# A recurrent attention layer on one core: two TensorE steps change places around the first chunk's scores

## The reference: what is computed

```python
h = rmsnorm(xn) * qkv_norm_w
q, k, v = split(h @ quantised(qkv_w).T)          # 16 heads of 64
for each chunk of T = 128 tokens:                # in order, with a state S per head
    scores = (q_i @ k_i.T) * mask                # decay mask, lower triangle
    o      = scale * (scores @ v_i + (q_i * lam_t) @ S)
    S      = lam_T * S + (k_i * lam_rev).T @ v_i
out = rmsnorm(rmsnorm(o) ...) @ quantised(proj_w).T
g   = silu(xn @ quantised(ffn_w).T + bias)
result = x + out * g
```

## Time and profile before

| | before |
|---|---|
| median of 3 runs | 1341.33 us (1341.18 to 1342.14) |
| the profiled execution: its own time | 1341.38 us |
| its span, first to last instruction | 1340.1 us |
| PE busy | 1312.0 us, 98% |
| DVE, POOL, ACT busy | 934.7, 635.5, 583.5 us |
| mean granted TensorE clock | 1.000 of full speed |

### The profile page before, as it was taken

How to read it: one execution, slowest core, us unless ns; L and a number is a source line. 1 busy time by engine, 2 the same in 40 slices (tenths; PEclk the granted TensorE clock), 3 DMA queues, 4 the chain that set the end, 5 groups by cost and what they waited for, 6 DMA issues and landing times.

```text
span 1340.1 us, 25937 instructions
## 1 busy us (share of the span) xinstructions
PE 1312.0 (98%) x10409; PEld 842.5 (63%) x10409; DVE 934.7 (70%) x1489; ACT 583.5 (44%) x1139; POOL 635.5 (47%) x532
## 2 busy tenths in 40 slices
PE   4999999999999999999999999999999999999998
PEld 2577767674656657566675656657566575656655
DVE  7887467785666957667575776957667686776835
ACT  5884143343434544444353434544344453434521
POOL 1432877952544535447341654535435352654432
PEclk9999999999999999999999999999999999999999
DMA  9521111203021030300303021030301303020000
GB/s 363 234 95 64 72 33 38 97 17 119 2 71 64 17 118 1 121 15 17 118 17 118 2 96 40 17 119 1 127 9 21 114 17 119 1 88 17 33 32 32
DMA packets 33432, 90.32 MB, mean 67 GB/s; under 512 B 10529, under 2 KB 10785, under 8 KB 33314
## 3 DMA queue, kind: packets, MB, share of 16 engines
q1 hardware_dynamic: 33024, 88.65, 18.7%
q10 hardware_dynamic: 290, 0.02, 0.0%
HBM read 71.85 MB, written 16.81 MB: 66 GB/s over the span
## 4 chain that ended last, share of the span: by engine, by line
PE 89%; POOL 3%; DVE 3%; ACT 2%; issue 2%; DMA 1%; SPq 0%; POOLq 0%; ACTq 0%; DVEq 0%
PE ring L747 19%; PE ring L880 15%; PE ring L706 13%; PE ring L732 12%; PE ring L680 11%; PE att_ps L784 4%; PE att_ps L830 3%; PE att_ps L834 3%; PE ring L796 2%; PE att_ps L811 2%; PE ring L759 1%; POOL sq L2186 1%; PE ring L655 1%; DMA raw<-in_ffn_w 1%; ACT junk L1700 1%
## 5 line engine op out<-in xcount | busy, mean ns | idle before, releaser
L747 PE MATMUL ring<-b_lo,qkv_q 128*128 128x256 f16 x1216 | 268.2, 273 | 0.0
L747 PE MATMUL ring<-b_hi,qkv_q 128*128 128x256 f16 x1216 | 268.2, 272 | 0.0
L880 PE MATMUL ring<-proj_q,o_hi 128*128 128x512 fp8e4 x496 | 188.1, 379 | 3.0 <-DVE o_lo L1422 3.0
L880 PE MATMUL ring<-proj_q,o_lo 128*128 128x512 fp8e4 x496 | 188.0, 379 | 0.0
L2142 POOL TENSOR_TENSOR gate_even<-gate_even,bias 128x512 f32<-128x512 f32 x14 | 19.8, 1414 | 275.4 <-ACT gate_even L1819 275.4
L2182 POOL TENSOR_TENSOR sq<-sq,cols 128x1024 f32<-128x1024 f32 x29 | 55.1, 1900 | 165.5 <-DVE b_lo L1254 157.3
L747 PEld LDWEIGHTS ring<-b_hi,qkv_q 128*128 128x128 fp8e4 x1216 | 120.3, 99 | 15.6
L747 PEld LDWEIGHTS ring<-b_lo,qkv_q 128*128 128x128 fp8e4 x1216 | 118.9, 98 | 15.7
L2208 POOL TENSOR_TENSOR xt<-xt,gate_even 128x512 f32<-128x512 f32 x58 | 88.2, 1531 | 69.7 <-DVE gate_even L1442 68.5
L2186 POOL TENSOR_TENSOR sq<-sq 128x1024 f32<-128x1024 f32 (+1 forms) x58 | 109.5, 1888 | 4.5
L1843 ACT ACTIVATE gate_even<-gate_even 128x512 f32<-128x512 f32 x60 | 37.6, 629 | 154.7 <-DVE gate_even L1285 154.7
(11 more groups left out here) (257 smaller groups left out, 3249.1 us busy)
## 6 DMA issues: line engine op xcount, KB each, us to landing
xt<-in_x SPq DMA_DIRECT2D x62, 512.0 KB, 8.3
out<-xt SPq DMA_DIRECT2D x31, 512.0 KB, 3.1
raw<-in_qkv_w SPq DMA_DIRECT2D x24, 512.0 KB, 15.7
y<-in_x_turned SPq DMA_DIRECT2D x14, 512.0 KB, 6.8
y_odd<-in_x_turned SPq DMA_DIRECT2D x14, 512.0 KB, 7.7
raw<-in_ffn_w SPq DMA_DIRECT2D x8, 512.0 KB, 9.9
norm_rows<-norm_out SPq DMA_DIRECT2D x14, 256.0 KB, 6.0
raw<-in_proj_w SPq DMA_DIRECT2D x6, 512.0 KB, 4.5
```

The costliest lines, as they stand in the source:

```text
L747: ins = pe.matmul(ring[:, b, e * BT:(e + 1) * BT], qkv_q[:, cb, o:o + P], part[:, cb, :], start=(cb == 0 and part is b_hi), stop=(cb == NC ...
L880: ins = pe.matmul(ring[:, b, :], part[:, cb, :], proj_q[:, cb, cs], start=(cb == 0 and k == 0), stop=(cb == NCB - 1 and k == 1))
```

## The change

Two calls in TensorE's program change their places in blocks 3 to 15; no instruction is added or taken away, and no other engine's program changes.

```diff
                 last = is_last(chunk(i, c))
                 scores(i, c)
                 if c == 0:
-                    v_product(i, "p4")
+
+                    turn_k(i, 1)
                     product(i, "p1")
-                    turn_k(i, 1)
                 else:
...
                 turn_k(i, 0)
                 v_product(i, "p3")
                 v_product(i, "p7")
+                v_product(i, "p4")
                 attention_by_tokens(i, 0)
                 attention_by_tokens(i, 1)
```

## The result

The changed kernel takes 1361.88 us (median of 5 runs, 1360.72 to 1364.09) against 1341.18 us for the kernel before on the same chip (5 runs, 1340.94 to 1342.14): a ratio of 1.0154, 95% interval 1.0142 to 1.0165. The forecast was 1358.3 us, with a range up to 1361.5. So the direction is right, and the time lies 0.4 us above the range and 3.6 us above the forecast. The profiled execution took 1361.88 us itself, 20.5 us more than that of before.

The account below looks back on a forecast made before the run. TensorE's list of matmuls was taken to set the time (busy 1312.0 of 1340.1 us). Hold 13.1, edges 0.1, POOL waits 2.6 and 1.1 made 16.9 us on 1341.4: 1358.3 us, range 1354 to 1361.5.

Parts of the forecast that it names:

- The hold at p4: TensorE's p4 right after p7 waits for DVE's add_v: 1.01 us in each of thirteen blocks, 13.1 us.
- The edges: TensorE's steps between kinds of matmul, p7 to outputs: 0.01 us a block, 0.1 us in all.
- POOL's chain: Later p1 delays sq_sum at L857: 2.6 us in three long waits, 1.1 us in six small ones.
- What I cost at nothing: Mask, ACT's take_v before the transposes' second half, and squares before chunk 1's scores: no new waits, 0 us.
- The sum: Whole kernel: 13.1 + 0.1 + 2.6 + 1.1 = 16.9 us on 1341.4, giving 1358.3 us, 1.3% slower.
- the hold is there: Denies the rival that ready scores pass the waiting p4 on TensorE, without hold: 1344.0 us, chance 0.03.
- the edges give nothing back: Denies the rival of scores beside transposes and p1 to outputs each 0.09 us cheaper: 1356.0 us, inside the range.
- the waits for `o_lo` are untouched: Denies the rival that the hold swallows TensorE's waits for o_lo and sq_sum: 1349.3 us, chance 0.04.
- POOL is late everywhere: Rival at L857: upper bound of POOL's chain, 6.2 us, with upper hold 14.3: 1362.0 us, chance 0.07.

Follow-up runs that it names:

- turning alone: Only the turning of k put ahead of p1, p4 left behind the scores, against the kernel before: 1353.35 us, ratio 1.0088.
- first try at a better version: Kernel before with POOL's sum_squares(i, 0) earlier, decay_state for chunk 1 behind output_scale(i, 0), and DVE's scale_o(i, 0) ahead of take_z21: 1345.94 us.
- before, squares first: Kernel before with POOL's squares of chunk 0 ahead of its decay of q for chunk 1, blocks from 3 on: 1345.07 us, ratio 1.0027.
- changed, squares first: Changed kernel with POOL's squares of chunk 0 ahead of its decay of q for chunk 1, blocks from 3 on: 1366.36 us, ratio 1.0185.
- before, second operation halved: Kernel before with two small POOL operations, the second at half its columns, ahead of sq_sum in blocks 4, 8 and 12: 1346.11 us, ratio 1.0037.
- `p4` alone, second operation halved: Kernel before with only p4 ahead of the scores, plus two small POOL operations, the second at half columns, ahead of sq_sum: 1362.14 us, ratio 1.0154.
- before, two small operations: Kernel before with two small POOL operations added ahead of sq_sum in blocks 4, 8 and 12: 1350.26 us, ratio 1.0058.

## Why the forecast was right in direction and too low in size

**The hold at p4** was right: 1.00 us in block 8 for 1.01, thirteen waits, 11.0 us of idle as foretold. Moving `p4` alone, which shifts no other wait, measured 13.5 us for the 13.1 of this term, inside its bounds.

**The edges** were mis-sized. Scores to transposes took the 1.99 us that I took, but the transposes behind the scores take 0.93 us in place of the 0.88 that they take behind a v product. With 1.06 us a block in all, hold and edges come to 13.8 us for 13.2.

**POOL's chain** was right, both for the three long waits (0.89 more each for 0.87) and for the six small ones (0.15 us for 0.18): 3.6 us for 3.7. Blocks 3, 7, 11 and 15 kept their margin.

**What I cost at nothing** held. The turning alone shows how near it was: without the scores as cover the wait for `take_v` costs 7 us.

**The sum** is the step that failed, by a term that it lacks. I let each wait cost what it lasts. I had read a granted clock of 1.00 and took it as given, while I put waits of 1.64 us in the place of waits of 0.77. After the longer ones the clock falls to a half for 3.41 us, in one to three blocks of a run, at 1.7 us each. In the changed kernel's five runs the clock shows one fall (1360.72 us), two (1361.50, 1361.88 and 1362.09) and three (1364.09). Take 1.7 us off for each, and the five are 1358.1 to 1359.0, against a forecast of 1358.3. The run with one fall lies inside the range, so it hung on the number of falls on which side of 1361.5 the median came.

That a longer wait at L857 does this is shown from both sides: lengthened without holds, it brings falls; shortened with all holds in place, the clock stays at 1.000 and the time drops by 7.0 us. None of the rivals came to pass: the hold is there, the edges give nothing back, the waits for `o_lo` are untouched, and POOL is late in six of the ten other blocks by 0.15 us, not in all. The measured time lies near that of "POOL is late everywhere" (1362.0) by accident; its reason is not in the trace.

Open is why one wait of 1.66 to 1.70 us is followed by a fall and the next is not, and whether the holds have a share at these lengths. What the runs show is how often. The table counts falls over all runs of a kernel, by clock and time; the waits are those of its profiled execution. Long waits had falls more often, and at about equal length the kernels with holds had more.

| kernel | waits | holds | falls, of waits |
|---|---|---|---|
| first try at a better version | 1.27 us at L880 | no | 0 of 28 |
| before, squares first | 1.54 us at L868 | no | 0 of 21 |
| changed, squares first | 1.55, 1.56 us at L868 | yes | 0 of 15 |
| turning alone | 1.64, 1.65 us at L857 | no | at most 2 of 12 |
| changed | 1.63, 1.66 us at L857 | yes | 10 of 15 |
| before, second operation halved | 1.66 to 1.70 us at L857 | no | 7 of 15 |
| `p4` alone, second operation halved | 1.68, 1.69 us at L857 | yes | 11 of 12 |
| before, two small operations | 1.83, 1.85 us at L857 | no | 13 of 15 |

## What to carry to other kernels

A product that adds into a bank which another engine still reads needs other work ahead of it: here the scores or `p1`, either of which hides what costs 13.5 us without it. When a reorder makes a wait of TensorE longer, look at what the granted clock does behind waits of that length, and count a fall as a term of its own. And a wait that a reorder of POOL takes away at one reader has to be followed to the next reader of the same chain, since it may only move there.

## What the chip did that I had not expected

TensorE's granted clock fell to 0.50 behind single waits of 1.66 to 1.85 us, in a program that had kept it at 1.00 from about 30 us on with waits of 0.77 us and also with thirteen more of 0.85 us. (The first products, up to 30 us, take 0.63 us each in the kernel before, the pace of a fall, though the clock column says 1.00 there too.) Each of the nine falls in the traces began 0.17 to 1.35 us after the waiting matmul's start and lasted 3.41 us, with matmuls of 0.63 us in place of 0.38, and cost 1.7 us, as much again as the wait before it. Transposes right behind matmuls on half of the array took 0.93 us for eight in place of 0.88.
